# Graph attention, 4096 rows on one core: 17 of 32 key blocks instead of 16 turned by DMA

## The reference: what is computed

```python
q = x @ Wq.T + bq;  k = x @ Wk.T + bk;  v = x @ Wv.T + bv
scores = q @ k.T / sqrt(128)
scores = where(adj > 0, scores, -9e15)      # adj: 4096 x 4096 int32
att = softmax(scores, axis=-1) @ v
out = layernorm(x + elu(att))               # over the 128 features, eps 1e-5
```

## Time and profile before

| what | value |
|---|---|
| median of 3 runs | 438.03 us (437.09 to 438.11) |
| the profiled execution, its own time | 437.68 us |
| its span in the trace | 435.8 us |
| TensorE busy | 423.3 us, 97% |
| VectorE, ScalarE, GpSimd busy | 83%, 82%, 79% |
| granted TensorE clock | 0.997 of full speed |
| DMA queue of SP | 104.41 MB, 90.1% of 16 engines |

### The profile page before, as it was taken

One profiled execution on the slowest core, in us unless ns is written; L12 is line 12 of the kernel. 1 busy time (PEld: TensorE's weight loads), 2 busy tenths in 40 slices (PEclk: granted clock), 3 DMA queues, 4 the chain that ended last, 5 costly groups with the idle time before them and its releaser, 6 DMA issues.

```text
span 435.8 us, 11401 instructions
## 1 busy us (share of the span) xinstructions
PE 423.3 (97%) x3479; PEld 310.6 (71%) x3479; DVE 362.9 (83%) x671; ACT 355.4 (82%) x737; POOL 343.6 (79%) x613
## 2 busy tenths in 40 slices
PE   8998999999999999999999999999999999999993
PEld 6563676777777777777777777777777777777783
DVE  1769987888899988888889888888889898888782
ACT  4778787888888988888888988888888988888991
POOL 0064568898888888898888988898888988888873
PEclk9999999999999999999999999999999999999998
DMA  8822999999999999999999999999999999998550
GB/s 226 376 98 97 205 250 270 266 271 283 277 262 272 258 249 275 266 262 250 264 278 262 262 246 274 266 266 255 252 279 262 269 247 265 267 264 197 102 105 18
DMA packets 149932, 104.76 MB, mean 240 GB/s; under 512 B 133024, under 2 KB 141728, under 8 KB 141728
## 3 DMA queue, kind: packets, MB, share of 16 engines
q1 hardware_dynamic: 149488, 104.41, 90.1%
q10 hardware_dynamic: 432, 0.20, 0.2%
HBM read 69.47 MB, written 2.10 MB: 164 GB/s over the span
## 4 chain that ended last, share of the span: by engine, by line
POOL 57%; issue 18%; PE 9%; DMA 6%; DVE 4%; POOLq 2%; ACT 2%; SPq 2%; DVEq 0%; ACTq 0%
POOL p_rows L320 25%; DMA p_turned<-p_rows 6%; POOL res L334 5%; POOL rstd L358 4%; POOL neg_mean L345 3%; POOL y L339 3%; POOL var L354 3%; POOL att_sum L327 3%; POOL att L329 3%; POOL centred L347 2%; POOL expm L336 2%; POOL var_eps L356 2%; DVE scores L587 2%; PE ps_t L716 2%; POOL y_out L362 2%
## 5 line engine op out<-in xcount | busy, mean ns | idle before, releaser
L320 POOL TENSOR_TENSOR p_rows<-scores,p_rows 128x256 f16<-128x256 f32 x252 | 175.8, 728 | 12.2 <-ACT p_rows L468 12.2
L587 DVE CUSTOM_DVE_ANT_0 scores<-ps_scores,adj 128x1024 f32<-128x1024 f32 x128 | 155.8, 1217 | 14.6 <-issue 10.8
L451 ACT ACTIVATE scores<-scores,neg_max 128x1024 f32<-128x1024 f32 x128 | 145.6, 1138 | 0.5 <-DVE neg_max L596 0.5
L602 DVE TENSOR_TENSOR p_lo<-ps_t,p_hi 128x512 f16<-128x512 f32 x124 | 82.5, 684 | 27.5 <-ACT p_hi L460 27.2
L573 DVE TENSOR_SCALAR adj<-adj 128x1024 f32<-128x1024 int32 x128 | 104.3, 815 | 0.7 <-DMA adj<-in_adj_dram 0.7
L776 PE MATMUL ps_scores<-k_hi,q_hi 128*128 128x512 f16 x256 | 97.1, 379 | 1.0 <-DVE max_parts L587 0.9
L777 PE MATMUL ps_scores<-k_lo,q_hi 128*128 128x512 f16 x256 | 97.0, 379 | 0.0
L778 PE MATMUL ps_scores<-k_hi,q_lo 128*128 128x512 f16 x256 | 97.0, 379 | 0.0
L815 PE MATMUL ps_out<-v_parts,p_hi 128*128 128x256 f16 x496 | 95.3, 273 | 0.7 <-DVE p_lo L602 0.5
L815 PE MATMUL ps_out<-v_parts,p_turned 128*128 128x256 f16 x496 | 95.0, 273 | 0.4 <-DMA p_turned<-p_rows 0.4
L817 PE MATMUL ps_out<-v_parts,p_lo 128*128 128x128 f16 x496 | 88.5, 219 | 0.0
(11 more groups left out here) (92 smaller groups left out, 474.3 us busy)
## 6 DMA issues: line engine op xcount, KB each, us to landing
adj<-in_adj_dram SPq DMA_DIRECT2D x64, 1024.0 KB, 5.3
out_dram<-y_out SPq DMA_DIRECT2D x32, 64.0 KB, 4.9
x_rows<-in_x_dram SPq DMA_DIRECT2D x4, 256.0 KB, 4.2
x_rows<-in_x_dram SPq DMA_DIRECT2D x2, 512.0 KB, 6.1
p_turned<-p_rows SPq DMA_TRANSPOSE x63, 4.5
w_rows<-in_L_gnn_Wq_dram ACTq DMA_DIRECT2D x1, 64.0 KB, 2.6
w_rows<-in_L_gnn_Wk_dram ACTq DMA_DIRECT2D x1, 64.0 KB, 3.3
w_rows<-in_L_gnn_Wv_dram ACTq DMA_DIRECT2D x1, 64.0 KB, 3.9
```

What stands on the lines that cost most here:

```text
L320: last = nc.gpsimd.tensor_tensor(p_rows[c][:, w:][:, cols], s_sb[s][:, c * PIECE:c * PIECE + w][:, cols], p_rows[c][:, 0:w][:, cols], ALU. ...
L451: nc.scalar.activation(s_sb[s][:, cols], s_sb[s][:, cols], ACT.Exp, bias=neg_max[:, s:s + 1], accum_out=p_sums[:, s, c:c + 1]).then_inc(ex ...
L587: nc.vector.tensor_tensor_reduce(out=s_sb[s][:, cols], in0=ps_scores[c % 2][:, :], in1=mask_sb[s][:, cols], scale=SCALE, scalar=-3.0e38, o ...
L602: nc.vector.tensor_tensor(p_lo[:, k, :], ps_t[bank_of(s, g)][:, :], p_hi[:, k, :], ALU.subtract).then_inc(plo_ready, 1)
```

## The change

`DMA_COLS` becomes (1024, 1152): the second turn takes nine blocks instead of eight, high and low, so 18 instead of 16. The ninth is block 0 of group 4. Group 4 stays a TensorE group with its other three blocks, so its transposes, `high_part` and `low_part` shrink from 512 to 384 columns, and `high_rows` and `low_rows` of c = 1 grow from 1024 to 1152 (each of the four GpSimd instructions from 256 to 288). `values` gets a ninth part, `TURNED_PART`, the one block from `p_turned[1]`, which runs in step 7 after group 3. The number of `values` matmuls is the same. The last tile keeps its own scheme: only its first turn is by DMA. The order of the instructions on SP, GpSimd, ScalarE and VectorE does not change; counts on semaphores follow the nine parts.

```diff
-DMA_COLS = (PIECE, PIECE)
+MIXED_COLS = 128
+DMA_COLS = (PIECE, PIECE + MIXED_COLS)
+MIXED = FIRST_PE
-PV_ORDER = (4, 5, 6, 0, 1, 7, 2, 3)
+TURNED_PART = STEPS
+PV_STEPS = ((4,), (5,), (6,), (0,), (1,), (7,), (2,), (3, TURNED_PART))
...
+        def by_pe(g):
+            return slice(MIXED_COLS, BANK) if g == MIXED else slice(0, BANK)
...
-                nc.scalar.activation(p_hi[:, k, :], ps_t[bank_of(s, g)][:, :], ACT.Copy).then_inc(phi_ready, 1)
+                nc.scalar.activation(p_hi[:, k, by_pe(g)], ps_t[bank_of(s, g)][:, by_pe(g)], ACT.Copy).then_inc(phi_ready, 1)
...
-                act.wait_ge(exp_done, exp_count(i, c))
+                act.wait_ge(exp_done, exp_count(i, (c * PIECE + w - 1) // PIECE))
...
-                    if c < BY_DMA:
-                        dve.wait_ge(rows_lo, BY_DMA * (i - 2) + c + 1)
+                    if 2 * c <= MIXED:
+                        dve.wait_ge(rows_lo, BY_DMA * (i - 2) + min(c + 1, BY_DMA))
...
-                for b in range(BLOCKS):
+                for b in range(by_pe(g).start // P, BLOCKS):
                     kb = g * BLOCKS + b
...
-                    if has_2:
-                        values(p - 2, n, PV_ORDER[j], first)
+                    for g in PV_STEPS[j]:
+                        if has_2:
+                            values(p - 2, n, g, first)
```

More of the change, by code:

```diff
@@ L20 @@
 LOG_P_SCALE = 15.0 * math.log(2.0)
-DMA_COLS = (PIECE, PIECE)
+MIXED_COLS = 128
+DMA_COLS = (PIECE, PIECE + MIXED_COLS)
 BY_DMA = len(DMA_COLS)
 FIRST_PE = sum(DMA_COLS) // BANK
+MIXED = FIRST_PE
 PE_GROUPS = STEPS - FIRST_PE
 T_AT = {4: 6, 5: 7, 6: 8, 7: 10}
-PV_ORDER = (4, 5, 6, 0, 1, 7, 2, 3)
+TURNED_PART = STEPS
+PV_STEPS = ((4,), (5,), (6,), (0,), (1,), (7,), (2,), (3, TURNED_PART))
+PV_ORDER = tuple(part for step in PV_STEPS for part in step)
+PV_PARTS = len(PV_ORDER)
 POOL_OPS = 11
@@ L200, in pv_count @@
         def pv_count(i, g):
-            return STEPS * i + PV_ORDER.index(g) + 1
+            return PV_PARTS * i + PV_ORDER.index(g) + 1
         def exp_count(i, c):
             return PIECES * i + c + 1
+        def by_pe(g):
+            return slice(MIXED_COLS, BANK) if g == MIXED else slice(0, BANK)
         def bank_of(s, g):
@@ L472, in attention @@
                 act.wait_ge(recip_ready, i + 1)
-                act.wait_ge(pv_done, STEPS * (i + 1))
+                act.wait_ge(pv_done, PV_PARTS * (i + 1))
                 nc.scalar.activation(att2[:, s, :], ps_out[s][:, 0:2 * D], ACT.Copy, scale=recip[:, s:s + 1]).then_inc(att_ready, 1)
@@ L495, in last_high_part @@
                 act.wait_ge(last_pt, g - LAST_PE + 1)
-                act.wait_ge(pv_done, STEPS * LAST)
+                act.wait_ge(pv_done, PV_PARTS * LAST)
                 nc.scalar.activation(last_high(g), last_ps[g], ACT.Copy).then_inc(last_hi_act, 1)
@@ L601, in low_part @@
                 dve.wait_ge(phi_ready, PE_GROUPS * i + k + 1)
-                nc.vector.tensor_tensor(p_lo[:, k, :], ps_t[bank_of(s, g)][:, :], p_hi[:, k, :],
+                nc.vector.tensor_tensor(p_lo[:, k, by_pe(g)], ps_t[bank_of(s, g)][:, by_pe(g)], p_hi[:, k, by_pe(g)],
                                         ALU.subtract).then_inc(plo_ready, 1)
@@ L614, in late_high_part @@
                 dve.wait_ge(pt_ready, PE_GROUPS * (LAST - 1) + k + 1)
-                dve.wait_ge(pv_done, STEPS * (LAST - 1))
+                dve.wait_ge(pv_done, PV_PARTS * (LAST - 1))
                 nc.vector.tensor_copy(p_hi[:, k, :], ps_t[bank_of(0, g)][:, :]).then_inc(phi_ready, 1)
@@ L793, in transposes, with values @@
                 last.then_inc(pt_ready, 1)
-            def values(i, s, g, first):
-                if g >= FIRST_PE:
+            def values(i, s, part, first):
+                g = MIXED if part == TURNED_PART else part
+                by_dma = part < FIRST_PE or part == TURNED_PART
+                c = min(g // 2, BY_DMA - 1)
+                if not by_dma:
                     pe.wait_ge(plo_ready, PE_GROUPS * i + g - FIRST_PE + 1)
-                elif g % 2 == 0 or pv_count(0, g - 1) > pv_count(0, g):
-                    pe.wait_ge(turned[g // 2], 16 * i + 16)
-                if g == PV_ORDER[0] and not first:
+                elif part % 2 == 0:
+                    pe.wait_ge(turned[c], 16 * i + 16)
+                if part == PV_ORDER[0] and not first:
                     pe.wait_ge(att_ready, i - 1)
@@ L805, in values @@
                     pe.wait_ge(v_lo, STEPS)
-                for b in range(BLOCKS):
+                turned_blocks = by_pe(g).start // P
+                blocks = range(turned_blocks) if part == TURNED_PART else range(turned_blocks, BLOCKS)
+                for b in blocks:
                     k = g * BLOCKS + b
-                    if g >= FIRST_PE:
+                    if by_dma:
+                        high = p_turned[c][s][:, k - c * PIECE // P, :]
+                        low = p_turned[c][s][:, DMA_COLS[c] // P + k - c * PIECE // P, :]
+                    else:
                         high = p_hi[:, g - FIRST_PE, b * P:(b + 1) * P]
                         low = p_lo[:, g - FIRST_PE, b * P:(b + 1) * P]
-                    else:
-                        high = p_turned[g // 2][s][:, g % 2 * BLOCKS + b, :]
-                        low = p_turned[g // 2][s][:, DMA_COLS[g // 2] // P + g % 2 * BLOCKS + b, :]
                     nc.tensor.matmul(ps_out[s][:, 0:2 * D], high, v_parts[:, k, :],
-                                     start=(g == PV_ORDER[0] and b == 0), stop=False)
+                                     start=(part == PV_ORDER[0] and b == blocks[0]), stop=False)
                     last = nc.tensor.matmul(ps_out[s][:, D:2 * D], low, v_parts[:, k, D:2 * D],
-                                            start=False, stop=(g == PV_ORDER[-1] and b == BLOCKS - 1))
+                                            start=False, stop=(part == PV_ORDER[-1] and b == blocks[-1]))
                 last.then_inc(pv_done, 1)
@@ L880, in _ @@
             last_transposes(3)
-            for g in (7, 2, 3):
+            for g in (7, 2, 3, TURNED_PART):
                 values(LAST - 1, 0, g, False)
```

## The result

The changed kernel takes 443.53 us in the median of 4 runs (442.81 to 444.51), the kernel before 437.95 beside it (437.09 to 438.11). The ratio is 1.0133, with a 95% interval of 1.0109 to 1.0157: slower by 5.6 us. The prediction said 443.0.

What follows compares the result with a forecast made beforehand. TensorE was taken as the bound, with a two-period loop through p_lo of group 5 level with it. Steady periods 3.7 + early clash 0.6 + early queue 1.0 = +5.3 us on 437.68 gave 443.0, range 437.0 to 447.0.

Steps and rivals of the forecast that it cites:

- The bound and the loop: TensorE bounds (12.22 of 12.23 us); a two-period loop through p_lo of group 5 is level, its TensorE part 0.056 longer.
- The clash: Period's end: mask op waits for GpSimd's fourth `low_rows` instruction, p_lo of group 5 0.26 later, +0.15 us per period; chance 0.66.
- GpSimd as a whole: GpSimd's period stays just inside: `low_rows` ends 0.34 us later, covered by `var`'s 0.72 wait for the mask op.
- ScalarE and VectorE: 128 columns move: `high_rows` +0.12 us, high part of group 4 -0.12, VectorE's p_lo of group 4 -0.13.
- The early queue: First four periods (44 to 95 us): 0.6 us from the clash, plus 1.0 (0 to 3) as SP's DMA queue drains more slowly.
- DMA later on: After 110 us the start's queue is worked off; steady DMA demand 12.3 of 12.38 us per period, still no stall.
- the demand of 12.3 us a period: Steady DMA time with the wider turn: 0.98 x 12.23 = 12.0 us, plus 0.3 to 0.4 for two blocks of 16.
- the DMA case: Rival: DMA bounds all through, turns land too late for `high_rows`, period 12.55, 447 to 449 us; chance 0.13.
- No clash: Rival: mask op and `low_rows` don't meet, or wider instructions cost little; loop -0.07 to +0.02, 437 to 438 us; chance 0.13.
- The gain arrives: Rival: TensorE's saved transposes count in full, 0.109 x 31 = 3.4 us, giving 434.3 us; chance 0.08.

Runs made afterwards that it cites:

- e5: Kernel before, with only one block of `values` of group 4 moved behind those of group 5: 440.88 us, ratio 1.0084.
- e3: Kernel before, with only GpSimd's four `low_rows` instructions of c = 1 widened to 288 columns, that low part left out of the result: 441.8 us, ratio 1.010.
- e1: Changed kernel, with the mask op of piece 2 moved from step 7 to step 1 of the next tile: 437.58 us, ratio 0.9994.
- e6: Changed kernel with the mask op moved as in e1, and half of each adjacency load left out after the first two tiles: 432.28 us, ratio 0.9887.
- e7: Changed kernel, with half of each adjacency load left out after the first two tiles: 441.47 us, ratio 1.0093.
- e4: Kernel before, with only the second turn widened to 18 blocks, two of them zeros nobody reads: 439.17 us, ratio 1.004.
- e8: Kernel before, with half of each adjacency load left out: 435.77 us, ratio 0.9966.
- e10: Kernel before, with GpSimd's wider instructions of e3 and the wider second turn of e4 together: 442.88 us, ratio 1.0135.
- e2: Kernel before, with the mask op of piece 2 moved from step 7 to step 1 of the next tile: 435.65 us, ratio 0.9963.
- e9: Changed kernel with the mask op moved as in e1, and each adjacency load issued ahead of the turn it had followed: 460.86 us, ratio 1.0538.

## Why the prediction was right, point by point

- **The bound and the loop.** Right. TensorE at 100% was no reason for a gain: a transpose less left the period longer, and e5 shows that sooner at p_lo of group 5 means waiting for it.
- **The clash.** Right in place, mechanism and size. `low_rows` takes 0.70 each as taken (2.82 us for four); the mask op waits for the fourth (1.05 us, forecast 1.0 to 1.2), and p_lo starts 0.52 after it. Counted from the end of GpSimd's `y`, p_lo of group 5 starts 4.86 us later, where it was 4.62 and 4.65 in turn: 0.22 more for the forecast 0.25. The steady loss was set at 0.15 x 25 = 3.7 and is 3.62. e3 makes nearly all of it alone, e1 and e6 take it away, e7 shows it without DMA pressure. What was left out is that it isn't always even: up to some 200 us short and long periods alternate (12.13, 12.66) with nearly the same mean; the mask op is held up in both, and TensorE stands still 0.55 us in the long ones, 0.02 in the short. And the sum's parts don't simply add: e3 alone gives 0.13 and e5 alone 0.11, the transpose less takes 0.055 off again (0.109 over two periods), which makes 0.185 where 0.145 was measured. No run took the rest apart. The 0.26 that TensorE stood still was set at 0.27; the period says 12.375 - 12.11 = 0.265.
- **GpSimd as a whole.** Right. It waits 0.19 us for `attention` in the even periods (0.33 and 0.52 in turn before), so it stays just inside and is not itself the bound. In the long ones of the alternating periods the wait is gone.
- **ScalarE and VectorE.** +0.12, -0.12 and -0.13, measured: `high_rows` 1.15 for 1.04, the high part of group 4 0.47 for 0.57, p_lo 0.56 for 0.69.
- **The early queue.** 0.6 + 1.0 was set for the four early periods, and they lost 1.47. e4 alone gives 1.1 of it. e7 against e8, the same step with a light queue, has early periods 50.52 - 49.95 = 0.57 longer, which is the 0.6 of the clash. Together that makes 1.7 for the measured 1.47. e3 doesn't fit: its early periods are not longer at all, but its start is late, and what its queue does with that wasn't tested.
- **DMA later on.** Wrong in part, and it cost the sum nothing. It said that the queue is worked off and there is still no stall. There is hardly a stall (e7's steady periods are no shorter than those of the changed kernel), but the queue is not worked off: share 1.05 for the forecast 1.0, issues of 4.3 to 5.6 us to the end. The step that failed is the demand of 12.3 us a period, taken from the added bytes: with the same bytes e10 has about 1.0 x 12.35 = 12.3, the changed kernel 1.05 x 12.375 = 13.0. I had named gaps at `high_rows` after 110 us together with issues above 5 us as the mark of the DMA case. Half of that came, every second issue is above 5 us, and no such gap. The slack that the prediction had read for the turns held, for landings 2.5 us later that it had not foreseen. By e1 and e6 this queue is what takes the gain once the clash is gone: the steady period goes from 12.22 to 12.10, 3.1 us over the 25.
- **The rivals.** "No clash" is what e1 comes nearest to. That it lies at 437.6, in the rival's 437 to 438, is luck: it is a mean of periods of 12.10 and of longer ones in which a load, a turn or p_lo is late, and the rival knew nothing of those. "The gain arrives" said 434.3 and needs e1's move and a lighter queue as well.

**What stays open.** Why the queue doesn't drain in the changed kernel and in e1. The bytes don't do it: e4 and e10 move the same 106.45 MB, and drain. What differs is how the engines' work lies between the turns (ScalarE's 1152 columns, shorter high parts, the order of `values`), and no run took these apart. One difference can be read: in every kernel whose queue drains a turn is issued 0.10 us after its rows are written, in the changed kernel 0.5 us on average in the steady periods and in e1 1.0. Whether that is what keeps the queue full or comes of it isn't shown. Also open is why e2's early periods are 1.5 us shorter with all loads in place: the mask op's later call on its load and the clashes of the earlier trace rows both go with that one move.

## What to carry to other kernels

Where an engine is 100% busy, follow the loops that return to it before counting a saving there: a second one of equal length takes the saving away, and the part that brings the engine sooner to its wait even turns it into a loss. GpSimd instructions that grow by an eighth in width can hold a VectorE instruction up by much more (here 0.07 us each made a mask op of 1.05 us out of one of 0.68); look at what was just missing them. And an operation that nobody waits for (here the mask for the next tile) doesn't belong ahead of one on the tightest chain: the move gained 0.4% in the kernel before (e2) and 1.3% in the changed one (e1), where the change alone lost 1.3%.

## What the runs showed of the chip that I had not expected

- The same transfers stand in the queue in two ways. Turns and loads with equal bytes and nearly equal periods go with a DMA share of 0.99 to 1.01 and turn issues of 3.1 us (e10) or with 1.05 to 1.07 and 4.3 to 5.6 us (the changed kernel), each to the end of the run.
- With each 1 MB load issued ahead of the transposing DMA on the same queue a period takes 13.07 us (e9), with the load behind it 12.22 (e1).
- The price when the mask op meets a GpSimd instruction is the rest of that instruction plus 0.51 to 0.52 us until VectorE's next one starts, in three kernels alike (before at 75 us, changed, e3). The Trainium skill has the lock (SBUF — State Buffer, "Who interferes with whom"), and these rows agree with it: whoever comes second blocks fully, and GpSimd's `var` in its turn takes 0.65 instead of 0.19.
